# Moving the low-part subtraction of the weight splitting from VectorE to GpSimd, in an attention and mixture-of-experts layer on eight cores

## The reference, cut to what matters

```python
xn = layernorm(x)                                  # x: (2, 8192, 1024), float32
q, k, v = (xn @ w_qkv.T)                           # 16 heads of 64
attn = softmax(einsum('bnhd,bngd->bnhg', q, k) / 8)   # heads against heads, within one token
o = einsum('bnhg,bngd->bnhd', attn, v).swapaxes(1, 2).reshape(b, n, d)
att = o @ w_proj.T + b_proj
routed = sum over e of cw[t, e] * relu(xn @ up[e].T)**2 @ down[e].T     # 8 experts, top 2
shared = relu(xn @ sup.T)**2 @ sdown.T
return x + att + routed + shared
```

## Time and profile before

| | us |
|---|---|
| median of 2 runs | 4255.03 (4250.59 to 4259.46) |
| profiled execution, its own time | 4240.39 |
| span of its slowest core (core 3) | 4238.8 |
| spans of the eight cores | 4205.5 to 4238.8 |
| mean granted TensorE clock, all cores | 0.851 to 0.856 |
| median span and clock, cores 0 to 3 | 4232.9, 0.852 |
| median span and clock, cores 4 to 7 | 4220.9, 0.853 |

### The profile page before, as it was taken

How to read it: one execution, slowest core, us unless ns; L and a number is a source line. 1 busy time by engine, 2 the same in 40 slices (tenths; PEclk the granted TensorE clock), 3 DMA queues, 4 the chain that set the end, 5 groups by cost and what they waited for, 6 DMA issues and landing times.

```text
span 4238.8 us, 47277 instructions; the slowest of 8 cores (4205.5 to 4238.8 us)
## 1 busy us (share of the span) xinstructions
PE 3361.9 (79%) x16592; PEld 1831.5 (43%) x16592; DVE 1028.6 (24%) x2190; ACT 581.5 (14%) x1190; POOL 153.2 (4%) x276
## 2 busy tenths in 40 slices
PE   4576757576656666659999969999879999899997
PEld 2354635353535454534444434444434444344443
DVE  3121121222222221142222331222322222312222
ACT  1120111121212120211100110011111110110010
POOL 1000010101010101000000000000000000000000
PEclk8668776868786868679999979999889999899998
DMA  5325272636364646432223222222322222322322
GB/s 152 126 83 145 74 237 96 210 118 213 125 212 129 200 141 194 143 109 91 85 90 112 72 105 100 105 94 96 115 75 95 95 80 95 105 85 94 110 87 92
DMA packets 172628, 506.89 MB, mean 120 GB/s; under 512 B 36056, under 2 KB 52568, under 8 KB 172384
## 3 DMA queue, kind: packets, MB, share of 16 engines
q1 hardware_dynamic: 121840, 415.69, 29.9%
q0 software_dynamic: 24832, 79.77, 5.2%
q10 hardware_dynamic: 25728, 8.39, 1.7%
HBM read 411.44 MB, written 75.50 MB: 115 GB/s over the span
## 4 chain that ended last, share of the span: by engine, by line
PE 67%; DMA 14%; DVE 6%; issue 5%; ACT 4%; ACTq 3%; SPq 0%; DVEq 0%; POOL 0%; POOLq 0%
PE p L284 58%; PE p L532 3%; PE p L514 3%; DMA wb<-sqk 3%; ACTq L425 2%; DMA ARB<-sv 2%; DMA wbig<-sproj 2%; DMA sdn_s<-ARB 2%; DMA sup_s<-ARB 2%; PE p L329 1%; PE p L868 1%; DVE ARB L262 1%; ACT AR L525 1%; ACT ARB L258 1%; DMA ssdn<-ARB 1%
## 5 line engine op out<-in xcount | busy, mean ns | idle before, releaser
L284 PE MATMUL p<-ARB,wb 128*128 128x512 bf16 (+1 forms) x7680 | 1518.7, 365 | 459.2 <-DMA wb<-sqk 204.8
L284 PEld LDWEIGHTS p<-ARB,wb 128*128 128x128 bf16 x7680 | 809.7, 107 | 1181.6 <-issue 584.3
L284 PE MATMUL p<-ARB,wbig 128*128 128x512 bf16 (+1 forms) x6144 | 1214.1, 361 | 89.1 <-DMA wbig<-sproj 34.3
L284 PEld LDWEIGHTS p<-ARB,wbig 128*128 128x128 bf16 x6144 | 611.3, 100 | 689.4 <-issue 127.7
L894 ACT ACTIVATE AR<-AR 128x512 f32<-128x512 f32 x128 | 80.6, 630 | 1197.9 <-DVE AR L889 1197.9
L284 PE MATMUL p<-ARB 128*128 128x512 bf16 x768 | 187.8, 402 | 53.7 <-DMA ARB<-sv 42.1
L930 DVE TENSOR_TENSOR AR<-p,AR 128x512 f32<-128x512 f32 x128 | 88.5, 692 | 528.8 <-PE p L284 511.2
L262 DVE TENSOR_TENSOR ARB<-AR,ARB 128x1024 bf16<-128x1024 f32 x96 | 117.6, 1225 | 345.5 <-ACT ARB L258 345.2
L532 PE MATMUL p<-AR 128*128 128x65 f32 x512 | 124.3, 422 | 78.3 <-ACT AR L525 78.3
L889 DVE TENSOR_SCALAR AR<-p 128x512 f32<-128x512 f32 x128 | 88.5, 692 | 351.3 <-PE p L284 351.3
L532 PEld LDWEIGHTS p<-AR 128*128 128x128 f32 x512 | 114.1, 328 | 95.2 <-issue 95.2
(11 more groups left out here) (89 smaller groups left out, 1185.3 us busy)
## 6 DMA issues: line engine op xcount, KB each, us to landing
wb<-sup_s SPq DMA_DIRECT2D x128, 512.0 KB, 4.4
wbig<-sdn_s SPq DMA_DIRECT2D x128, 512.0 KB, 3.3
wb<-sqk SPq DMA_DIRECT2D x112, 512.0 KB, 7.3
wb<-ssup SPq DMA_DIRECT2D x64, 512.0 KB, 4.2
wbig<-ssdn SPq DMA_DIRECT2D x64, 512.0 KB, 4.0
ARB<-sv SPq DMA_DIRECT2D x56, 512.0 KB, 4.2
wbig<-sproj SPq DMA_DIRECT2D x56, 512.0 KB, 4.0
AR<-wup SPq DMA_DIRECT2D x32, 512.0 KB, 6.0
```

What stands on the lines that cost most here:

```text
L284: E.matmul(psum_ap, wa, xa_, start=(first_flag and i == 0), stop=(stop_flag and i == 2)),
```

## The change

In `presplit` the subtraction goes from VectorE's list to GpSimd's, with the same operands, and signals a new semaphore "P". It still waits for the ScalarE cast. The store's issue on GpSimd waits for it, now on the same engine. The index of the float32 slot and that of the bfloat16 slot get separate names, both still pi % 2. `t_wsf_prev` becomes a list of four, of which two are used. `outp` moves from a tensor of its own into the arena, behind `xres` (floats 19200 to 21248), and the arena grows from 20064 to 21280 floats. `load_w`, which splits the attention weights in iteration 0, is unchanged and keeps its VectorE subtraction.

```diff
-        outp = _st.enter_context(nc.sbuf_tensor("outp", [128, 2 * 1024], F32))
...
-        ARF = 20064
+        ARF = 21280
...
         xres, _ = take(128, 2 * 1024)
+        outp, _ = take(128, 2 * 1024)
...
-        t_wsf_prev = [None, None]
+        t_wsf_prev = [None] * 4
...
         def presplit(fp32_src, scratch_blk, pi):
             fs = pi % 2
+            ps = pi % 2
             W("sync", t_wsf_prev[fs])
             dfi = bd.do("sync", lambda E, fs=fs, src=fp32_src:
                         E.dma_start(out=wsf[:, 1024 * fs:1024 * fs + 1024],
                                     in_=src), "F%d" % fs, 16)
-            W("scalar", dfi, t_spl_scrw[fs])
-            thi = bd.do("scalar", lambda E, fs=fs:
-                        E.copy(spl[:, 2048 * fs:2048 * fs + 1024],
+            W("scalar", dfi, t_spl_scrw[ps])
+            thi = bd.do("scalar", lambda E, fs=fs, ps=ps:
+                        E.copy(spl[:, 2048 * ps:2048 * ps + 1024],
                                wsf[:, 1024 * fs:1024 * fs + 1024]), "S", 1)
-            W("vector", thi)
-            tlo = bd.do("vector", lambda E, fs=fs:
-                        E.tensor_sub(spl[:, 2048 * fs + 1024:2048 * fs + 2048],
+            W("gpsimd", thi)
+            tlo = bd.do("gpsimd", lambda E, fs=fs, ps=ps:
+                        E.tensor_sub(spl[:, 2048 * ps + 1024:2048 * ps + 2048],
                                      wsf[:, 1024 * fs:1024 * fs + 1024],
-                                     spl[:, 2048 * fs:2048 * fs + 1024]), "V", 1)
+                                     spl[:, 2048 * ps:2048 * ps + 1024]), "P", 1)
             t_wsf_prev[fs] = tlo
             W("gpsimd", tlo)
...
```

More of the change, by code:

```diff
@@ L178, in build_nc @@
         semnames = ["I", "X", "W0", "W1", "W2", "W3", "WV0", "WV1", "B0", "B1",
-                    "SHQ", "SHK", "PV", "PV2", "O0", "O1", "F0", "F1", "SW0", "SW1",
-                    "XR0", "XR1", "G0", "G1", "T", "V", "S"]
+                    "SHQ", "SHK", "PV", "PV2", "O0", "O1",
+                    "F0", "F1", "SW0", "SW1",
+                    "XR0", "XR1", "G0", "G1", "T", "V", "S", "P"]
         sems = {k: _st.enter_context(nc.semaphore("s" + k)) for k in semnames}
@@ L255, in presplit @@
                                     in_=src), "F%d" % fs, 16)
-            W("scalar", dfi, t_spl_scrw[fs])
-            thi = bd.do("scalar", lambda E, fs=fs:
-                        E.copy(spl[:, 2048 * fs:2048 * fs + 1024],
+            W("scalar", dfi, t_spl_scrw[ps])
+            thi = bd.do("scalar", lambda E, fs=fs, ps=ps:
+                        E.copy(spl[:, 2048 * ps:2048 * ps + 1024],
                                wsf[:, 1024 * fs:1024 * fs + 1024]), "S", 1)
-            W("vector", thi)
-            tlo = bd.do("vector", lambda E, fs=fs:
-                        E.tensor_sub(spl[:, 2048 * fs + 1024:2048 * fs + 2048],
+            W("gpsimd", thi)
+            tlo = bd.do("gpsimd", lambda E, fs=fs, ps=ps:
+                        E.tensor_sub(spl[:, 2048 * ps + 1024:2048 * ps + 2048],
                                      wsf[:, 1024 * fs:1024 * fs + 1024],
-                                     spl[:, 2048 * fs:2048 * fs + 1024]), "V", 1)
+                                     spl[:, 2048 * ps:2048 * ps + 1024]), "P", 1)
             t_wsf_prev[fs] = tlo
             W("gpsimd", tlo)
-            t_spl_scrw[fs] = bd.do("gpsimd", lambda E, fs=fs, dst=scratch_blk:
+            t_spl_scrw[ps] = bd.do("gpsimd", lambda E, ps=ps, dst=scratch_blk:
                                    E.dma_start(out=dst,
-                                               in_=spl[:, 2048 * fs:2048 * fs + 2048]),
-                                   "SW%d" % fs, 16)
+                                               in_=spl[:, 2048 * ps:2048 * ps + 2048]),
+                                   "SW%d" % ps, 16)
         def wsl(buf, sl, kc, lo=False):
```

## The result

| | before | changed |
|---|---|---|
| median, us | 4258.08 (14 runs) | 4275.92 (15 runs) |
| ratio, changed to before | | 1.0046, 95% interval 1.0033 to 1.0059 |
| mean span of the eight cores in the profiled execution | 4226.3 | 4255.0 |
| spans of the cores | 4205.5 to 4238.8 | 4225.9 to 4285.2 |

The change costs about 20 us, 0.46% (14 to 25 us by the interval). That is clear of noise and well within 2%. 4281 us was predicted, a ratio of 1.006.

The account below looks back on a forecast made before the run. Bound: latency on the q/k stages' chain, no engine full. 35.1 + 3 - 2.5 = 35.6 us, 5.9 an iteration, cut by DMA give-back to 4.2, 25.5 in all: ratio 1.006, median 4281 us, range 4240 to 4330.

Parts of the forecast that it names:

- Where it is bound: Whole kernel: no engine is full; chain latency counts, with splitting setting the pace in q/k stages a = 2 to 7.
- The subtraction: Each split job: 2.27 us on GpSimd against VectorE's 1.225, adding 1.05 us; ends kept at 1.225 and 3.34.
- The hand-overs: Cast to subtraction to store issue: +0.42 us ahead, 0.26 saved behind, net +0.16 us per subtraction.
- rival C: Split jobs: the 0.52 us issue lag vanishes and GpSimd matches VectorE, up to 17 us faster, median 4238; chance 0.14.
- Together: Per subtraction on the chain: 1.05 plus 0.16 gives 1.21 us, times 29 full subtractions 35.1 us.
- The stage's start: First job of each of six q/k stages: store goes out some 0.5 us later, +3 us in all.
- The stage's end: Five stage ends: VectorE evacuates transposes about 1 us sooner, 0.5 us of it counted, -2.5 us in all.
- cap by the head shift: Stage's end: the head shift lands at 881.3, so the gain ends near 881.7, where matmuls began at 882.43.
- The DMAs' give-back: Longer q/k stages lower DMA share and landing times, cutting 5.9 us an iteration to 4.2, 25.5 in all.
- VectorE's relief elsewhere: q evacuations no longer behind a subtraction: costed at nothing, hidden by weight loads; otherwise a gain in blocks 0 to 7.
- Rival A: q/k stages: DMAs give nothing back and the clock costs 5 us more, 41 us in all, median about 4296; chance 0.16.
- Rival B: GpSimd becomes the bound if a subtraction takes over 5 us: 82 us, median 4337; at 6 us, 4358; chance 0.08.

Follow-up runs that it names:

- three samples of before: Sums of the six q/k stages: kernel before 532.5 us, with only `outp` moved to the arena 536.9, with only each stage's last subtraction on GpSimd 539.0.
- the two kernels with four slots: Four bfloat16 slots in place of two, `outp` in the arena: subtraction on GpSimd 4243 us (one execution), on VectorE ratio 0.9959 to the kernel before.
- the two with both edits: Four bfloat16 slots and next block's weight load ahead of the float32 load: ratio to the kernel before 0.9797 with VectorE's subtraction, 0.9826 with GpSimd's.
- the weights first: Subtraction on VectorE, two bfloat16 slots, next block's weight load issued ahead of the float32 load and head shift: ratio 0.9939 to the kernel before.
- the loads issued by GpSimd: Subtraction on VectorE, two slots, GpSimd instead of SP issues job n+2's float32 load behind job n's store: ratio 1.005 to the kernel before.

## Why the prediction was right

The time, 4276 us, lies 5 us from the 4281 predicted, the sign and the main mechanism (latency on the chain of the q/k stages) are those predicted, and the range held it. The cost itself was predicted at 25.5 us and measured at 20 (14 to 25). Several terms were off, partly in opposite ways, so that the match of the two times is closer than the working deserved, and in part luck.

- **Where it is bound: right.** The q/k stages carry it, GpSimd is not the bound, busy shares say nothing.
- **The subtraction: 2.27 us taken, 2.116 measured.** The added duration is 0.89 us, not 1.05. The Trainium skill's factor of 1.96 (GPSIMD Engine Reference, section 3) gave an estimate of 2.40; here it is 2.116 / 1.225 = 1.73 (the Trainium skill's factor is for float32 alone and 2048 columns).
- **The hand-overs: +0.16 us taken, +0.07 measured, both halves wrong.** I thought GpSimd's 0.52 us were the price of waiting for another engine and would move ahead of the subtraction. They didn't: GpSimd starts computing 0.15 us after the cast, against VectorE's 0.10, and the 0.5 us stayed ahead of the store's issue although it waits for its own engine. The gain of rival C, whose point was that this lag would vanish, was therefore not there.
- **Together 1.21 us taken, 0.95 measured**: the stages' sum before relief should have been 29 x 0.95 + 3 = 30.6 us, not 38.
- **The stage's start: +0.5 us taken.** In the changed kernel the first cast of a = 3 starts at 790.22 (core 1) and the store goes out at 794.09, 3.87 us; before, 788.54 - 785.12 = 3.42 (core 3). Over all 48 starts it is 3.87 against 3.34 us, +0.53: right.
- **The stage's end: -0.5 us taken, -0.93 measured.** The mechanism was right, its cap by the head shift too strict: the matmuls start 0.93 us sooner, as much as VectorE does.
- **The DMAs' give-back: the landings fell as worked out, what it gave back is open.** The weight loads' median landing, mean over the cores, fell from 7.73 to 7.45 us, and that of the stores to `sup_s` from 7.49 to 7.25: 0.28 and 0.24 us, where 0.055 x 4.2 = 0.23 was worked out. But the landings on the chains hardly fell: on average a core's chain holds 41.1 of them in the six stages before and 41.3 after, of 7.52 and 7.47 us each. The stages' sum can't decide it: with the whole give-back they should have grown by 30.6 / 1.39 = 22.0 us, with none by 30.6, and they grew by 22.9 to 29.4, depending on which of the three samples of before is taken.
- **VectorE's relief elsewhere: nothing taken; not borne out.** The prediction said that a gain in blocks 0 to 7 would speak against it. The changed kernel costs 5 to 8 us there and 18 to 21 in blocks 8 to 15, though the chains hold about as many subtractions in the one half as in the other (17.6 and 17.4 pieces before, 17.9 and 18.1 after, the starts included). In blocks 0 to 7 VectorE's q evacuations take 10.0 us of a core's chain before and 4.2 after. So some relief seems to be there, and the k blocks cost more than was counted, and in the sum the two hide one another. Between the two kernels with four slots the move costs 9.8 and 13.2 us, and between the two with both edits 2.6 and 11.2: less in blocks 0 to 7 each time. No run isolates the cause, and it stays open.

In short, at the measured latency the prediction's own terms give 30.6 - 4.6 = 26 us without the give-back, and 26 / 1.39 = 19 with it. The time of the whole kernel rose by 20 us (14 to 25). If the give-back is real, the smaller latency and the larger gain at the end account for the 5 us by which the prediction was too high. If it isn't, 26 us is just above what was measured, and its absence made up for what the other two took off. The runs don't decide between the two.

Rival A (no give-back, and a clock that costs more) is undecided in its mechanism, but its price of 41 us is twice what was measured. Rival B was far off: it took two subtractions in a row to bring GpSimd near the bound.

## What to carry to other kernels

Moving an instruction to an idle engine is paid by latency, not by load: count how often it stands on the chain, and multiply by the change in time from what releases it to what it releases. Where two loops of nearly the same length pace a stage, opening one shows only part of its worth; loosening both here gave 95 us of stage time where each alone gave 30. And before a job is shared between VectorE and GpSimd, check that the two can run at the same time: here a subtraction with two inputs in SBUF, divided between them, ran one part after the other and gained nothing.

## What the runs showed of the hardware that I had not expected

- GpSimd issued a DMA 0.54 us after its own subtraction had ended, about as long as after VectorE's (0.52 us), while SP went on after 0.08 us and ScalarE's cast released GpSimd's computing within 0.15 us. In these kernels the lag belongs to GpSimd's issue, not to the hand-over.
- A two-input subtraction on GpSimd and one on VectorE, started 0.05 us apart, ran one after the other: 0.907 us became 1.54.
- The same sixteen scatters took ScalarE's queue 12.1, 15.5 and 16.8 us to issue in three kernels (the kernel before, the weights first, the loads issued by GpSimd). The DMA share in these stretches was 0.81, 0.91 and 0.85, so it doesn't follow the share alone. The cause stays open.
